# A graph attention kernel on one core: GpSimd's first gather of a pair also waits for a signal of TensorE

## The reference

```python
Q, K, V = (x @ Wq), (x @ Wk), (x @ Wv)            # 8 heads of 64
score = einsum('ehd,ehd->eh', K[src], Q[dst]) / sqrt(64)
score = exp(clip(score, -5, 5))[..., None]
wV = segment_sum(V[src] * score, dst)
Z = segment_sum(score, dst)
h = x + (wV / (Z + 1e-06)).reshape(N, D)
h = (h - mean(h, 0)) * rsqrt(var(h, 0) + 1e-05) * gamma + beta
out = layernorm(x + h)
```

## Time and profile before

| | |
|---|---|
| time, median of 3 runs | 2098.77 us (2097.2 to 2105.61) |
| the profiled execution, its own time | 2113.25 us |
| its span, first to last instruction | 2111.5 us |
| TensorE busy | 1918.3 us, 91% |
| VectorE busy | 1696.9 us, 80% |
| ScalarE busy | 1377.7 us, 65% |
| GpSimd busy | 1249.1 us, 59% |
| mean granted TensorE clock | 0.990 |
| edge stage, by the first and the last multiply | 463.9 to 1959.1 us |

### The profile page before, as it was taken

One profiled execution on the slowest core, in us unless ns is written; L12 is line 12 of the kernel. 1 busy time (PEld: TensorE's weight loads), 2 busy tenths in 40 slices (PEclk: granted clock), 3 DMA queues, 4 the chain that ended last, 5 costly groups with the idle time before them and its releaser, 6 DMA issues.

```text
span 2111.5 us, 41623 instructions
## 1 busy us (share of the span) xinstructions
PE 1918.3 (91%) x7904; PEld 1351.1 (64%) x8014; DVE 1696.9 (80%) x2454; ACT 1377.7 (65%) x4602; POOL 1249.1 (59%) x1473
## 2 busy tenths in 40 slices
PE   7999999989998998998899899898899899899887
PEld 4555555547776776776677677676676677677433
DVE  6676655538888888888888888888888888888988
ACT  0001000018887887887888888788788788788866
POOL 0106663026666666666666666666666666666657
PEclk9999999999999999999999999999999999999999
DMA  4648886358998898888888989898899899889607
GB/s 172 176 147 299 293 301 237 143 206 300 315 326 291 304 322 307 313 305 309 306 307 305 325 315 311 301 314 300 296 321 309 294 317 320 307 300 331 225 0 289
DMA packets 184521, 589.09 MB, mean 279 GB/s; under 512 B 28480, under 2 KB 30240, under 8 KB 184480
## 3 DMA queue, kind: packets, MB, share of 16 engines
q0 software_dynamic: 135904, 465.14, 63.5%
q1 hardware_dynamic: 45120, 121.69, 16.2%
q10 hardware_dynamic: 3456, 1.78, 0.3%
HBM read 535.27 MB, written 78.91 MB: 291 GB/s over the span
## 4 chain that ended last, share of the span: by engine, by line
PE 70%; DVE 16%; issue 7%; another core or an unknown queue 2%; ACT 2%; DMA 1%; POOL 1%; SPq 0%; DVEq 0%; ACTq 0%; POOLq 0%
PE q_ps L915 26%; PE places L342 20%; PE acc L940 19%; DVE kv L791 11%; PE mm_ps L925 2%; DVE stats L1278 1%; DVE agg L1262 1%; ACT agg L1189 1%; DVE raw L802 1%; PE mm_ps L927 1%; DVE agg L1271 1%; PE places L402 1%; PE banks L1132 1%; DMA kv<-kv_d,idx 1%
## 5 line engine op out<-in xcount | busy, mean ns | idle before, releaser
L747 POOL DMA_INDIRECT kv<-kv_d,idx x880 | 891.9, 1014 | 548.9 <-issue 214.0
L842 ACT ACTIVATE kv<-kv 128x64 f32<-128x64 f32 x3520 | 888.9, 335 | 14.3
L940 PE MATMUL acc<-kv,mm_sb 128*128 128x260 f32 x3520 | 852.1, 385 | 11.9 <-issue 4.4
L940 PEld LDWEIGHTS acc<-kv,mm_sb 128*128 128x128 f32 x3520 | 672.8, 192 | 114.3 <-issue 10.7
L791 DVE TENSOR_TENSOR kv<-q_ps,kv 128x1024 f32<-128x1024 f32 x440 | 536.4, 1219 | 214.7 <-PE q_ps L915 161.1
L915 PE MATMUL q_ps<-q_tile,mm_sb 128*128 x1760 | 550.0, 434 | 146.0 <-DVE kv L791 114.7
L802 DVE TENSOR_REDUCE raw<-kv 128x16 f32<-128x1024 f32 x440 | 532.7, 1211 | 0.0
L915 PEld LDWEIGHTS q_ps<-q_tile,mm_sb 128*128 128x128 f32 x1760 | 316.9, 190 | 285.3 <-DVE kv L791 193.6
L852 ACT ACTIVATE mm_sb<-mm_ps,less 128x1024 fp32r<-128x1024 f32 x220 | 241.5, 1098 | 66.2 <-remote 60.1
L710 DVE TENSOR_TENSOR kv<-kv 128x384 f32<-128x384 f32 (+1 forms) x440 | 271.8, 618 | 0.0
L856 ACT ACTIVATE kv<-raw 128x16 f32<-128x16 f32 x440 | 92.0, 209 | 197.9 <-DVE raw L795 181.8
(11 more groups left out here) (171 smaller groups left out, 1354.1 us busy)
## 6 DMA issues: line engine op xcount, KB each, us to landing
q_tile<-q_d SPq DMA_DIRECT2D x49, 512.0 KB
kv<-kv_d,idx POOLq DMA_INDIRECT x880
kv_d<-kv_a SPq DMA_DIRECT2D x25, 512.0 KB
xb<-in_x POOLq DMA_DIRECT2D x49, 256.0 KB, 4.2
xb_d<-xb POOLq DMA_DIRECT2D x49, 256.0 KB, 3.7
out_rows<-agg SPq DMA_DIRECT2D x49, 256.0 KB, 2.1
x_sb<-in_xT SPq DMA_DIRECT2D x24, 512.0 KB, 8.1
q_d<-q_a SPq DMA_DIRECT2D x24, 512.0 KB
```

What stands on the lines that cost most here:

```text
L747: pool.indirect_dma_start(kv[:, s, u, 0:2 * DIM], None, kv_d, bass.IndirectOffsetOnAxis(idx[:, s, u:u + 1], 0), bounds_check=N_NODES - 1, ...
L842: return act.activation(v, v, ACT.Copy, scale=kv[:, s, u, 2 * DIM + h:2 * DIM + h + 1])
L940: last = pe.matmul(acc[:, bass.ds(par, 1), DIM - (1 - n) * HALF:DIM + n * HALF], m, kv[:, sc, u, DIM + n * HALF:DIM + (n + 1) * HALF], sta ...
```

## The change

The first gather of each pair gets one more wait. Besides the free place in the ring it waits until `s_qx` has reached q-2, that is until TensorE has signalled the Q of pair q-3. For the first three pairs the value is zero or less and nothing is waited for.

```diff
-        POOL_LAG = 5
+        POOL_LAG, Q_LAG = 5, 3
@@
                 if u == 0:
                     if s % IDX_PAIRS == 0:
                         wait_apart(pool, s_idx[s // IDX_PAIRS], fills)
                     wait_apart(pool, s_seg[s], fills - 1)
+                    wait_apart(pool, s_qx, q + 1 - Q_LAG)
                 pool.indirect_dma_start(kv[:, s, u, 0:2 * DIM], None, kv_d,
```

## The result

| | before | after |
|---|---|---|
| median of the runs | 2097.98 us (2095.6 to 2105.61, 4 runs) | 2116.46 us (2115.22 to 2119.91, 4 runs) |
| ratio, 95% interval | 1 | 1.0084 (1.0056 to 1.0113) |
| profiled execution, span | 2111.5 us | 2118.0 us |
| edge stage, first to last multiply | 1495.2 us | 1494.2 us |

The change makes the kernel slower by 0.8%, 18 us, where 193 were forecast. Between the two profiled executions the edge stage differs by 1 us: that of before took 2113.25 us, some 15 above its median, that of after 2119.91, 3.5 above its own.

A forecast was written before the change was run, and what follows sets the result against it. It took a TensorE-VectorE ring of 6.63 us a turn as the bound. The new ring, 3.83 + 3.77 = 7.60 over 219.5 turns, plus half of 40 us disturbances, gave 193 us more: 2290 us, range 2105 to 2430.

The forecast's parts named there:

- The ring: Edge stage: Q signal, two gathers, GpSimd's weighing, TensorE's sums, next Q; 3.83 us from signal to sums, turn 7.60 us.
- The step that failed: Edge stage, TensorE: from the start of the sums to the next signal of Q, 3.77 us, late signal included.
- the lag of 0.91: Edge stage: Q matmuls end at 1206.91, VectorE sees the signal at 1207.82; cause unknown, lag kept in the new turn.
- Rival 1: Q's signal stops being late, the lag coming from work piled up on TensorE: turn 6.72, 2080 to 2120 us; 14%.
- GpSimd does not bound this turn: Edge stage before the change: four gathers and a weighing leave GpSimd 1.24 us idle before pair p+6's first gather.
- H: Later theory, not in the prediction: TensorE's signals are held until about 1.9 us after GpSimd's last gather starts.
- The two stretches of the earlier trace: Edge stage, sums' start to next signal: 4.58 us after TensorE waited for its sums' data, 2.89 without lag elsewhere.
- the disturbed turns of before: Edge stage: turns averaged 6.81 us against a plain 6.63; 40 us in all, half expected to remain.
- Rival 3: Faster: signal on time and gathers no longer piling up at the DMA engines, so disturbances go; 2079 us; 5%.
- Rival 4: Gathered data come too late, so multiplies wait 0.7 to 1.7 us more a turn: 2440 to 2660 us; 4%.
- The gathers held by VectorE's weighing (2410): One moved gather a turn waits out VectorE's two-input weighing: turn 0.55 us longer, near 2410 us; 3%.
- the prediction's median "says no": Edge stage: 822 gathers had a median of 998 ns beside such weighings, taken as evidence against held gathers.

The follow-up runs named there:

- e13: The changed kernel with GpSimd weighing two heads of even pairs instead of one: 2159.86 us, 1.1298 of the kernel before on the same chip.
- e1: The changed kernel with GpSimd's weighing moved ahead of its two gathers in odd steps, new wait kept: 2092.08 us, 0.9967 of the kernel before.
- e11: The changed kernel with all of the weighing done by VectorE, none by GpSimd: 2085.85 us, 0.9931 of the kernel before.
- e4: The kernel before, with TensorE waiting for its own even Q signal ahead of the odd sums: 2137.49 us, 1.0174.
- e6: The kernel before, with TensorE waiting for its own odd Q signal ahead of the even sums, behind the one-hot matmuls: 2091.66 us, 0.997.
- e10: The kernel before, with plain copies of the same bytes from fixed rows in place of GpSimd's indirect gathers: 1902.19 us, 0.9059.
- e16: The changed kernel, unchanged, profiled on another chip: 2113.7 us, 1.1058 of the kernel before on that chip.
- e15: The kernel before, unchanged, profiled on another chip: 1912.32 us.
- e8: The changed kernel with the new wait in even pairs only: 2114.42 us, 1.0081 of the kernel before.
- e9: The kernel before, with all of the weighing done by VectorE, none by GpSimd: 2116.21 us, 1.0086.
- e12: The kernel before, with GpSimd weighing two heads of even pairs instead of one: 2080.95 us, 0.9924.
- e14: The changed kernel with GpSimd's weighing ahead of its two gathers and two heads weighed instead of one: 1977.84 us, 1.036 of the kernel before.
- e7: The changed kernel with the new wait on the Q of the pair two back instead of three: 3177.0 us in one execution.

## Why the prediction was wrong

**The ring.** The wait does close the ring, through each member named: 0.82 + 1.30 + 1.01 + 0.42 + 0.28 = 3.83 us. That the sum met the forecast's to the hundredth is partly luck: its first member was a choice of 0.8 between 0.3 and 1.0. e13 shows that it is the ring which bounds the turn: one member made 0.21 longer, the turn 0.22.

**The step that failed** is the other half: "From the start of the sums to the next signal of Q the row has 1214.45 - 1210.68 = 3.77, the 0.91 of the late signal included." It measured 2.96: the lag of 0.91 that this term carries over was not there. Rival 1, at 14%, is what happened, and its sum (a turn of 6.72, 2080 to 2120) held the time. Its reason, work piled up on TensorE, is not shown: e1 and e11 fit it, e4, e6 and e10 don't. I had written that I did not know what held the signal, and carried it over as if it belonged to TensorE's work. That 2116.46 lies inside the stated range of 2105 to 2430 is no merit of the forecast's sum; the range's lower end was rival 1's.

**A second slip** stands earlier: "GpSimd does not bound this turn." Its 1.24 us of idle time was taken as slack, and the sums of p-2 as just done when its gather began. They had ended 1.77 us before its wait did. If H is right for the kernel before, GpSimd's gathers and this wait are the ring of 6.64 us.

**What I weighed against rival 1 was weak.** The two stretches of the earlier trace rows seemed to contradict each other. Each has gathers beside it (before, GpSimd and TensorE in order of time):

```profile
1340.47 1.28 PE L915 MATMUL q_ps<-q_tile,mm_sb 128*128 x4
...
1341.61 0.99 POOL L747 DMA_INDIRECT kv<-kv_d,idx  x1 [0.30 <-issue]
1342.63 0.41 POOL L710 TENSOR_TENSOR kv<-kv 128x128 f32<-128x128 f32 x1
```
```profile
1669.97 1.25 POOL L747 DMA_INDIRECT kv<-kv_d,idx  x1 [0.30 <-issue]
...
1670.21 1.29 PE L915 MATMUL q_ps<-q_tile,mm_sb 128*128 x4
...
1671.53 0.99 POOL L747 DMA_INDIRECT kv<-kv_d,idx  x1 [0.30 <-issue]
```

In the first the Q ends at 1341.75, a last gather starts at 1341.61, and the multiply 1.87 after it: a release like that of the table. In the second the Q ends at 1671.50, 1.53 after a gather's start, and the next gather follows at once: on time. Both fit the gathers' timing, so what told them apart need not be the sums' data, as the prediction took it; two cases prove neither.

**Why the signal is on time after the change.** This is argued, and in part open. The wait ties GpSimd to the signal. The gathers of the turn start at fixed distances behind it, and the last one 1.67 us ahead of the end of the next even Q (1204.21 to 1205.88), where 1.00 was usual. With a release at 1.9 that leaves a lag of 0.2 instead of 0.9, most of what is missing. It does not explain why nothing is left: of the Qs that ended 1.5 to 1.8 us after the start of a last gather 5 of 187 were late in the changed kernel, and 117 of 143 in the other traces with late signals. The odd Q ends 0.56 after a gather's start and is on time too; there the next gather starts 1.6 after that start. In e11, where none follows for 2.3 us, 71 of 74 in that place were late.

**Why only 18 us are left of it.** Where signals are late the changed kernel has a turn of 3.83 + 2.96 = 6.79 against a median of 6.67 that was itself full of late signals. Over the stage the disturbed turns of before make up the difference: the mean is 6.81 in both. Between the medians of the runs 18 us remain.

**What the price is without the late signals.** On the chip of e16 the change costs 201 us, a stage of 1492.9 against 1292.1. The 193 forecast is near that by accident: I had put 0.81 us too much in the new turn (7.60 for 6.79), and the turn of before, 6.63, holds 0.80 more than 5.83.

**The rest.** Rival 3 came by half. The disturbed turns did go, 219.5 turns of 6.79 are 1490 us of a stage of 1494; but the new ring, at 6.79 and not the 6.72 that it was priced with, took the gain. That less piling up at the DMA engines did it is not shown: their share was 0.89 before and after. Rival 4 did not come: the multiplies waited 2.9 us in all for gathers. The gathers held by VectorE's weighing (2410) did not come: all 205 moved first gathers between 500 and 1900 us overlap that weighing, with a median of 991 ns, and none takes over 1100. All 880:

```profile
L748 POOL DMA_INDIRECT kv<-kv_d,idx x880: 986/995/1548, 459.8 to 1957.2; - x176
```

Yet single gathers do seem to be held. Of those over 1100 ns in this stretch, 21 before and 7 after (38 in e15, 10 in e16), every one overlapped a weighing of VectorE; of the 1496 gathers of these four traces that overlapped none, none took over 1046. That the prediction's median "says no" is right for the price and not for every gather.

What holds the signals, and why in some measurements only, stays open. The release, 1.9 us after a gather's start, comes 0.9 after its recorded end. The Trainium skill says of that record that it ends before GpSimd is through ("Perfetto Trace Analysis", section "DMA Instruction — SWDGE (GPSIMD)": the end shown is the last descriptor written, and the processor completes the instruction later). No run here shows what GpSimd does in those 0.9 us, and the traces without late signals have the same record.

## What to carry to other kernels

A lag that no row explains is an unknown with two ends, zero being one of them; it may depend on the very timing that the change moves, and here on the chip or the occasion. Profile the kernel before on a second chip before pricing a change of 1% against it: the same edit cost 0.8% on one and 10.6% on the other. A ring of work and known gaps can be summed well from single held cases; test it by making one member longer, as e13 did.

## What the runs showed of the hardware

- **Signals of TensorE seen late after a gather.** In the twelve traces with late signals (before and after, e1 to e6, e8, e9, e11, e12), between 500 and 1900 us, 1228 Qs ended 0.7 to 1.5 us after the start of a gather with no other gather within 1.8 us of that start. 1202 of these were late. They were seen 1.91 us after that start in the median. Of 183 that ended 2 us or more after a gather's start none was late, and of 1921 with a next gather within 1.5 us 89 were. e11 shows that the 1.9 is not a constant: there 71 late ones were seen at 1.56.
- **Two other chips did not show it.** In the four traces of e13 to e16 none of 1533 Qs was late; 133 of them ended in that same place, 108 of these in e14, so e14 is the trace that tests it. The kernel before took 2098 to 2100 us in the first measurement and on three chips, and 1911.66 and 1911.79 on two others, at granted clocks of 0.990 and 0.995. Each of these five chips was measured on one occasion, and the two without late signals came last, so the chip and something that changed with time are not told apart.
- **A signal of TensorE and a GpSimd wait.** GpSimd's own wait for TensorE's sums was late by 1.8 us in the turn of the earlier trace rows, so the lateness is not VectorE's.
- **Gathers and VectorE's weighing.** Every gather over 1100 ns (76 in before, after, e15 and e16) overlapped a VectorE operation with two inputs in SBUF; most gathers that overlap one are not longer.
- **Long pauses cost twice.** With 0.71 us a turn before the sums the granted clock stayed at 1.00, and so it did with 0.92 in e13; with 3.40 (e7) it was 0.79 over the stage, and the same eight matmul records took 3.83 us instead of 2.02.
